# A scan layer on one core: softplus by ScalarE, two of sixteen products on GpSimd, state sums in four 32-column tiles

## The reference

```python
xz = xs @ W_in;  xi, z = split(xz)
xc = silu(causal_conv4(xi) + conv_b)
dt_r, Bc, Cc = split(xc @ W_x, [2, 2 + 16])
dt = softplus(dt_r @ W_dt + b_dt)
A = -exp(A_log)
def step(h, (x_t, dt_t, B_t, C_t)):
    h = exp(dt_t[:, None] * A) * h + dt_t[:, None] * B_t[None, :] * x_t[:, None]
    return h, sum_s(h * C_t)
y = scan(step) + xc * D_skip
out = x + (y * silu(z)) @ W_out
```

## Time and profile before

| | us |
|---|---|
| median of the runs (3133.92 to 3143.5) | 3143.29 |
| profiled execution, first to last instruction (span) | 3123.6 |
| scan layer, from its first scan to its last product with C | 1295.6 to 3113.0 |
| share of the span busy: PE, DVE, POOL, ACT | 82%, 80%, 66%, 61% |

### The profile page before, as it was taken

One profiled execution on the slowest core, in us unless ns is written; L12 is line 12 of the kernel. 1 busy time (PEld: TensorE's weight loads), 2 busy tenths in 40 slices (PEclk: granted clock), 3 DMA queues, 4 the chain that ended last, 5 costly groups with the idle time before them and its releaser, 6 DMA issues.

```text
span 3123.6 us, 40760 instructions
## 1 busy us (share of the span) xinstructions
PE 2573.1 (82%) x12954; PEld 756.1 (24%) x12954; DVE 2485.6 (80%) x2176; ACT 1914.4 (61%) x2402; POOL 2065.3 (66%) x1284
## 2 busy tenths in 40 slices
PE   5888878888788775688888888888888888888886
PEld 1233123331233211222222222222222222222221
DVE  5655656555555544599999999999999999999998
ACT  4534654346543343667777777677777776777772
POOL 2543245432444313298898888988988889889886
PEclk9999999999999988799999999999999999999999
DMA  4797327863279647667677677676775766767765
GB/s 162 241 325 212 102 67 255 294 205 102 72 241 313 192 133 181 132 146 181 147 165 167 144 177 163 148 181 148 162 170 145 179 160 148 180 148 162 171 145 117
DMA packets 257701, 537.53 MB, mean 172 GB/s; under 512 B 39608, under 2 KB 150656, under 8 KB 256688
## 3 DMA queue, kind: packets, MB, share of 16 engines
q1 hardware_dynamic: 215328, 444.01, 53.7%
q0 software_dynamic: 19040, 64.24, 7.7%
q10 hardware_dynamic: 23216, 27.74, 3.7%
HBM read 396.55 MB, written 139.33 MB: 172 GB/s over the span
## 4 chain that ended last, share of the span: by engine, by line
POOL 29%; issue 27%; PE 5%; DVE 2%; DMA 2%; ACT 1%; SPq 1%; POOLq 0%; ACTq 0%; DVEq 0%
POOL m_hs L500 18%; POOL m_sp_v L517 2%; POOL m_dtx L527 2%; POOL m_gated L506 2%; DMA t_tile<-band_out 1%; POOL m_dt L524 1%; POOL m_dt L520 1%; SPq L913 1%; DVE m_pb L472 1%; PE t_bank L1096 1%; PE t_bank L1057 1%; PE t_bank L1021 1%; POOL t_xc L1481 1%; DVE m_hs L477 1%; PE m_misc L230 0%
## 5 line engine op out<-in xcount | busy, mean ns | idle before, releaser
L500 POOL TENSOR_TENSOR m_hs<-m_hs,m_cs 128x1024 f32<-128x1024 f32 x512 | 1203.6, 2358 | 288.4 <-DVE m_hs L477 288.4
L477 DVE TENSOR_TENSOR_SCAN m_hs<-m_da,m_pb 128x1024 f32<-128x1024 f32 x512 | 1170.7, 2287 | 29.3 <-ACT m_da L399 4.2
L399 ACT ACTIVATE m_da<-m_dtb,m_a_neg 128x1020 f32<-128x1020 f32 x512 | 576.6, 1144 | 275.9 <-DMA m_dtb<-dt_rows 254.1
L282 PE MATMUL m_pb<-m_dtx,late 64*128 64x512 f32 x2048 | 583.5, 646 | 150.2 <-DVE m_hs L477 146.9
L265 PE MATMUL m_py<-m_hs,late 128*64 128x512 f32 x2048 | 565.8, 631 | 104.8 <-POOL m_hs L500 104.0
L472 DVE TENSOR_TENSOR m_pb<-m_pb,m_bs 128x1024 f32<-128x1024 f32 x512 | 619.7, 1210 | 20.9 <-PE m_pb L282 20.9
L1481 POOL TENSOR_TENSOR t_xc<-t_xc,big 128x512 f32<-128x512 f32 x96 | 120.1, 1271 | 338.8 <-DVE big L1387 338.8
L282 PEld LDWEIGHTS m_pb<-m_dtx,late 64*128 64x128 f32 x2048 | 163.4, 188 | 567.3 <-DVE m_hs L477 457.5
L1021 PE MATMUL t_bank<-late,t_lwin 128*128 128x256 f32 x816 | 217.3, 404 | 63.3 <-ACT big L1260 34.0
L1359 DVE SCALAR_TENSOR_TENSOR t_xc<-t_bank,t_vec,t_xc 128x512 f32<-128x512 f32 x96 | 72.0, 750 | 244.2 <-PE t_bank L1057 244.2
L1248 ACT ACTIVATE t_sq<-t_bank 128x512 f32<-128x512 f32 x192 | 105.5, 598 | 245.3 <-PE t_bank L1096 245.2
(11 more groups left out here) (166 smaller groups left out, 3591.3 us busy)
## 6 DMA issues: line engine op xcount, KB each, us to landing
m_dtb<-dt_rows SPq DMA_DIRECT2D x512, 512.0 KB, 6.1
late<-right_factor POOLq DMA_DIRECT2D x102, 512.0 KB, 5.5
right_factor<-t_tile SPq DMA_DIRECT2D x192, 256.0 KB, 3.5
t_tile<-band_out SPq DMA_DIRECT2D x183, 256.0 KB, 4.2
band_out<-t_vwin SPq DMA_DIRECT2D x48, 512.0 KB
...
```

Source lines behind the costliest of these rows:

```text
L282: m = nc.tensor.matmul(pb[s % 2][:, half(n)], spread[rows, dg, :], dtx[par][rows, half(q)], start=True, stop=True)
L399: nc.scalar.activation(da[:, s % DA_RING, :, 1:T], dtb[s % DTB_RING][:, :].rearrange("p (r t) -> p r t", t=T)[:, :, 1:T], ACT.Exp, scale=a ...
L477: nc.vector.tensor_tensor_scan(hs[:, s % H_RING, :], da[:, s % DA_RING, :, :].rearrange("p r t -> p (r t)"), pb[s % 2][:, :], 0.0, ALU.mul ...
L500: nc.gpsimd.tensor_tensor(hs[:, s % H_RING, :], hs[:, s % H_RING, :], cs[q][:, :], ALU.mult).then_inc(hc_ready, 1)
```

## The change

Seven things change, all in the scan layer; the loop is also written out (no hardware loop).

1. Softplus is one ACT function (table set "softplus"), two half operations per chunk straight from PSUM to `dt`. The Abs/Exp/Ln/Identity/Relu operations and POOL's six half operations go.
2. In steps 5 and 15 of each chunk (`POOL_U`) DVE makes no product. PE spreads dt*x into `misc` ("u5", "u15"), ACT copies it to SBUF (`ub`), POOL multiplies it by B. The decay of such a step is written into the PSUM tile `pb[1]`, free in that step, instead of `da`; its first column is zeroed by a tiny ACT copy. So the scan reads one operand from PSUM and one from SBUF, as before.
3. The channel groups run in the order `DGS = (0, 4, 1, 5, ...)`, and the sums of two steps are made together, in four 32-column tiles of PE (`sum_two`). `H_RING` is 6, `LAG` 5.
4. The residual input is added by PE (a matmul with the identity `eye` into `py[1]`); ACT copies the sum to `fin`. DVE has no more `fin`.
5. Decays are made two steps ahead (`AHEAD = 2`), but those of steps 5 and 15 one step ahead, since they must wait until the scan two steps earlier has left `pb[1]`.
6. z comes before dt, and its two halves use different rows of PE, so they can run side by side. On ACT, the shared work of a step now stands ahead of the step's decay.
7. SP issues the stores of dt and of the output between its loads.

```diff
-    DA_RING = H_RING = 4
-    LAG = 3
+    DA_RING = 4
+    H_RING = 6
+    LAG = 5
+    AHEAD = 2
+    DGS = (0, 4, 1, 5, 2, 6, 3, 7)
+    POOL_U = (5, 15)
...
         SHARES = {
-            "tensor": {0: [(PRE, "x")], 2: [(OWN, "bq1")], 4: [(OWN, "cq1")], 5: [(PRE, "dt")],
-                       8: [(PRE, "z"), (POST, "out")], 9: [(PRE, "bq0")], 11: [(PRE, "cq0")]},
+            "tensor": {0: [(OWN, "u5")], 1: [(OWN, "bq1")], 2: [(OWN, "cq1")], 4: [(PRE, "x0")], 5: [(PRE, "x1")],
+                       6: [(PRE, "z")], 8: [(PRE, "dt")], 9: [(POST, "out")], 10: [(OWN, "u15")], 12: [(PRE, "bq0")], 14: [(PRE, "cq0")]},
...
+                elif op[0] == "u":
+                        q, i = divmod(int(op[1:]), DG)
+                        dg = DGS[i]
...
+                            nc.tensor.matmul(misc[n][:, :], spread[rows, dg, :], dtx[par][rows, half(q)],
+                                             start=True, stop=True).then_inc(misc_ready[n], 1)
...
-                    pe.wait_ge(hc_ready, g + 1)
+                    pe.wait_ge(hc_ready, g + 2)
                     for n in range(2):
-                        m = nc.tensor.matmul(py[q][D * n:D * n + D, :], gather[:, dg, :], hs[:, s % H_RING, half(n)],
-                                             start=False, stop=(dg == DG - 1), skip_group_check=True)
-                    m.then_inc(hc_used, 1)
+                        for two in range(2):
+                            strip, dg = divmod(DGS[i + two], DG // 2)
+                            o = D * n + D // 2 * strip
+                            m = nc.tensor.matmul(py[q][o:o + D // 2, :], gather[:, dg, :], hs[:, (g + two) % H_RING, half(n)],
+                                                 start=False, stop=(i == DG - 2), skip_group_check=True)
+                            if n == 1:
+                                m.then_inc(hc_used, 1)
...
+                    elif op == "dt":
+                        a.preload_act_table_set("softplus")
...
+                            nc.scalar.activation(dt[:, half(q)], misc[q][:, :], ACT.Softplus, bias=b_dt).then_inc(misc_used[q], 1)
+                        a.preload_act_table_set("natural_log_exp_and_others")
...
+                    if s in POOL_U:
+                        a.wait_ge(h_ready, g - 1)
+                        to = pb[s % 2][:, :].rearrange("p (r t) -> p r t", t=T)
+                        nc.scalar.copy(to[:, :, 0:1], zeros[:, :].unsqueeze(2))
...
+                    if s in POOL_U:
+                        j = pool_products(k, s)
+                        v.wait_ge(ub_ready, j + 1)
+                        decays, products = pb[s % 2][:, :], ub[j % UB_RING][:, :]
```

More of the change, by code:

```diff
@@ new lines, in mamba_layer @@
+            "scalar": {1: [(OWN, "u5")], 2: [(OWN, "bq1")], 3: [(OWN, "cq1")], 4: [(POST, "take1")], 6: [(PRE, "silu")],
+                       9: [(PRE, "dt")], 10: [(POST, "fin")], 11: [(OWN, "u15")], 12: [(OWN, "take0")], 13: [(PRE, "bq0"), (NEXT2, "xg0")],
+                       15: [(PRE, "cq0"), (NEXT2, "xg1")]},
+            "vector": {},
+            "gpsimd": {1: [(OWN, "u5")], 3: [(POST, "gate1")], 9: [(PRE, "dtx0")], 10: [(PRE, "dtx1")], 11: [(OWN, "u15")],
+                       13: [(OWN, "gate0")]},
@@ L180, in schedule @@
-        def schedule(eng, name, pre, steps, post):
+        FIRST = {"vector": {9: [(PRE, "dtx0"), (PRE, "dtx1")]}, "gpsimd": {}}
+        def schedule(name, pre, steps, post):
             def share(k, par, kinds, s):
-                table = FIRST if kinds == (PRE,) and k == -1 and name in FIRST else FIRST_X if isinstance(k, int) and k == -2 and name in FIRST_X else SHARES
+                table = FIRST if kinds == (PRE,) and k == -1 and name in FIRST else FIRST_X if k == -2 and name in FIRST_X else SHARES
@@ L277, in steps @@
+                    dg = DGS[i]
+                    if i == 0:
                         pe.wait_ge(dtx_ready, 2 * k + q + 1)
-                    if not (first and s < 2):
-                        pe.wait_ge(h_ready, g - 1)
-                    for n in range(2):
-                        rows = slice(D * n, D * n + D)
-                        m = nc.tensor.matmul(pb[s % 2][:, half(n)], spread[rows, dg, :], dtx[par][rows, half(q)],
-                                             start=True, stop=True)
@@ L284, in steps @@
-                    m.then_inc(b_ready, 1)
-                    if s >= LAG:
-                        sum_states(k, par, s - LAG)
-                    elif not first:
-                        sum_states(k - 1, 1 - par, S - LAG + s)
+                    if s not in POOL_U:
+                        if not (first and s < 2):
+                            pe.wait_ge(h_ready, g - 1)
+                        for n in range(2):
+                            rows = slice(D * n, D * n + D)
+                            m = nc.tensor.matmul(pb[s % 2][:, half(n)], spread[rows, dg, :], dtx[par][rows, half(q)],
+                                                 start=True, stop=True)
+                        m.then_inc(b_ready, 1)
@@ L413, in post @@
                         return take(k, par, 1)
-                    a.wait_ge(fin_done, k + 1)
-                    for g in range(G):
-                        a.dma_start(out[:, bass.ds(SUB * k + g * NG, SUB), :],
-                                    fin[DM * g:DM * g + DM, :].rearrange("p (n t) -> p n t", n=SUB)).then_inc(stored, 16)
-                schedule(a, "scalar", pre, steps, post)
+                    a.wait_ge(o_ready, k + 1)
+                    if not early(k, 1):
+                        a.wait_ge(stored, 16 * G * k)
+                    nc.scalar.copy(fin[:, :], py[1][:, :]).then_inc(fin_done, 1)
+                schedule("scalar", pre, steps, post)
             @block.vector
```

330 lines of the change are left out of this document (145 added, 185 removed).

## The result

The changed kernel takes 3003.03 us (median of 4 runs, 2997.88 to 3006.89), the kernel before 3142.78 beside it: ratio 0.9562, 95% interval 0.9545 to 0.958, faster by 140 us. In a later series of runs it was 3004.88 against 3136.06: 0.9584, 0.9559 to 0.9608, 131 us. The forecast was 3022, its range 3000 to 3072.

A forecast was written before the change was run, and what follows sets the result against it. DVE was taken as the bound, busy 98% of the scan stage. 79.4 + 29.8 + 21.4 - 15.5 + 7 - 1 = 121 us off the 3123.6 us span gives 3003; plus 19.7 around it, 3022 us, range 3000 to 3072.

The forecast's parts named there:

- rival (1): Main forecast: DVE stays the bound and stalls 0 to 1.3 us per chunk, 3006 to 3047 us; chance 0.66.
- Products: 2 of 16 products leave DVE in each of 32 chunks: 64 x 1.24 = 79.4 us saved.
- Stalls: DVE's waits in the scan stage: today's 21.4 us replaced by 0.5 per chunk end, 15.5 us.
- Head: Ahead of the first scan, softplus in one piece brings the first decay 7 us sooner, at most 10, at least 0.
- E3: End of step 3's scan; the first chain, from there to step 7's `pb`, takes 8.7 us, DVE 9.0: fits by 0.3.
- E13: End of step 13's scan; the second chain, to the next chunk's step 2 `pb`, takes 12.0 us, DVE 12.4: fits by 0.4.
- SP: Store of dt and next chunk's first load queue on SP; counted as nothing, but if late, the chain from E13 is too.
- The clock: PE idles some 3.5 us per chunk end, its clock falls in most chunks; step 0's `pb` stalls DVE 0 to 0.7 us.
- (2): The chains from E3 and E13 lose: DVE waits in every chunk; 3053 to 3100 us, chance 0.20.
- (3): Lone scans, with decay in PSUM or POOL's product late, lose what their product saved: 3101 us; chance 0.05.
- (4): Slower than before by PE's clock: at three quarters of the time at 1.2 GHz, 3463 us; chance 0.04.
- (5): Better than the sum: no stalls and the full 10 us at the head, down to 3003 us; chance 0.05.

The follow-up runs named there:

- the filler: Changed kernel plus three 512-column matmuls, results overwritten, in PE's wait at the chunk's end: 2997.67 us, ratio 0.9564, chunk 52.60 instead of 52.87.
- experiment 3: Changed kernel plus one 512-column ACT copy ahead of silu's table switch: stage 1715.45 us; then also the identity matmul moved ahead of z: stage 1690.92.

## Why the prediction was right, and where it was off

**The forecast's time was 19 us too high by one step**: "The span has 19.7 us around it to the median of 3143.29, and I keep these." Around a span lie 1.9 us (3133.0 beside 3134.88, 3003.4 beside 3005.28). So the other 17.8 us are no fixed cost: the profiled execution was a short one (some 3125.5 us by the same 1.9), its layer beginning at 1254.60 where all others but one begin at 1259 to 1268, and the median of three was high: 11 later runs of the same kernel have a median of 3135.86, another 11 one of 3136.06. What makes the stretch ahead vary was not tried. The span itself was forecast as 3003 and measured as 3003.4, but this is partly luck: my sum was 121 us, the layer became 128.7 us shorter, and it started 8.5 us later. The range, too, held the time by 3 us only: 3003 lies below the 3006 at which rival (1), the main forecast, begins.

**The sum, term by term.** The stage became 1812.66 - 1690.93 = 121.7 us shorter, 115.1 forecast.
- Products, 79.4 forecast: undoing them cost 73.1 and removed the stall at the chunk's end, worth some 8; without stalls on either side it is 2.53 per chunk against 2.48. Right.
- `fin`, 29.8: undoing it cost 27.4, and 0.96 per pass at its place. Right.
- Stalls, 21.4 less 15.5: the mis-sized term. The 511 distances from the first scan to the last, with 64 products less, are 1681.4 us; 1690.93 leaves 9.5, where I had 15.5. By the same count the kernel before has 22.0. The clock's part is 0.29 us at 28 of 31 chunk ends, 8 us, and the filler takes all of it; some 1.6 lie in the first chunk and 1.0 at step 10 of the last. (These come to some 1 us more than 9.5, because the product behind a lone scan costs 0.02 less than the count has it, 63 times.)
- Head, 7: from the layer's start to the first scan 41.01 became 32.63, 8.4. The first scan came at 1295.70, not near 1289, since the layer started later.
- Tail, 1: from the last scan's start to the end 15.3 became 16.8, 1.5.

The parts that were undone are worth 73.1 + 27.4 + 11.0 = 111.5 of the 121.7 us, if they add up. What removed the stalls that the kernel before has between scans 0 and 1 of a chunk (3.99 us on the mean, where 3.45 is the step) was not tried: softplus in one piece, decays two steps ahead, the order of z and dt, and the stores on SP were never undone alone.

**The chains.** The first ran from E3 at 1890.84 to the projection of step 7 at 1898.95, 8.1 us against 8.7 forecast, and DVE came at 1899.83, 9.0 as forecast. The second ran from E13 at 1871.15 to the projection of step 2 at 1882.86, 11.7 against 12.0, with DVE there 12.7 after E13. Neither makes DVE wait. The loads, the risk named under *SP*, came in time: ACT's waits for `dtb` fell from 254.1 us in all to 2.4.

**The clock.** A gap of 3.5 us and a fall in most chunks were forecast, a stall of 0 to 0.7; measured 4.00, nearly every chunk, 0.26 on average (3.68 against 3.42 between scans 15 and 0). Right. For z I saw the danger, "up to 1.5 us, in perhaps one chunk of five"; the changed kernel has none of it, and experiment 3 shows that 0.5 us more of waiting brings it, at up to 1.4 us in three chunks of four. The reading behind it, that the gaps of 1.31 and 1.11 us in the earlier trace rows "were enough", did not carry over: waits of 1.3 and 1.5 us in the changed kernel cost nothing, so what else led to the fall in the earlier trace rows stays open.

**The rivals.** (1) held in its mechanism; its time, 3006 to 3047, was missed by 3 us, through the 19.7 above. (2) did not happen, but its mechanism, the clock down ahead of z, is real and half a microsecond away. (3) was wrong for the operands as they lie, and half right for another choice: from SBUF alone the lone scans cost 0.25 to 0.44 us more each. (4) was far off: mean clock 0.95. (5), 3003 without stalls and with the full head, was hit in time, for another reason. Of the four signs of being wrong none came: a chunk is 52.87 us, a lone scan 2.265, DVE never waits for `ub` or `hs`, and ACT hardly for `dtb`.
